# Deformable attention held by rows of four lines, with results and inputs moved during the loop and far lists regrouped through memory

## What is computed

```python
v = xt @ value_proj_w.T + value_proj_b
om = xt @ offset_mask_w.T + offset_mask_b
...
loc_x = px + DIL * kx + off[..., 0] * OFFSET_SCALE
loc_y = py + DIL * ky + off[..., 1] * OFFSET_SCALE
...
sampled = corner(y0i, x0i, (1 - wy) * (1 - wx)) + corner(y0i, x0i + 1, (1 - wy) * wx) + corner(y0i + 1, x0i, wy * (1 - wx)) + corner(y0i + 1, x0i + 1, wy * wx)
...
out = jnp.einsum('nhwkgc,nhwkg->nhwgc', sampled, mask_t)
out = out.reshape(N, L, C) @ output_proj_w.T + output_proj_b
```

## Time and profile before

| | us |
|---|---|
| median of 3 runs | 3287.48 (3285.68 to 3289.9) |
| profiled execution | 3290.47 |
| its span | 3288.8 |

### The profile page before, as it was taken

How to read it: one execution, slowest core, us unless ns; L and a number is a source line. 1 busy time by engine, 2 the same in 40 slices (tenths; PEclk the granted TensorE clock), 3 DMA queues, 4 the chain that set the end, 5 groups by cost and what they waited for, 6 DMA issues and landing times.

```text
span 3288.8 us, 77998 instructions
## 1 busy us (share of the span) xinstructions
PE 2733.5 (83%) x22424; PEld 2192.2 (67%) x22424; DVE 2719.8 (83%) x6553; ACT 1828.7 (56%) x3486; POOL 1162.0 (35%) x1557
## 2 busy tenths in 40 slices
PE   1888889999999999995677989998946799999986
PEld 0555555565565556564566888887835688888885
DVE  3888888888888888885667999999945799999996
ACT  0888888888888888884143443333202443334420
POOL 3333233333333333332446231346232441115550
PEclk9999999999999999998988999999978899999998
DMA  7889897888888898895553233333374433333334
GB/s 182 158 157 163 166 148 138 139 140 143 138 141 142 141 139 143 140 144 116 183 158 91 89 99 101 99 103 84 89 261 134 144 101 101 97 101 95 102 89 160
DMA packets 351779, 432.59 MB, mean 132 GB/s; under 512 B 42352, under 2 KB 275200, under 8 KB 346480
## 3 DMA queue, kind: packets, MB, share of 16 engines
q1 hardware_dynamic: 339696, 423.85, 58.5%
q0 software_dynamic: 11904, 6.44, 1.5%
HBM read 283.33 MB, written 147.09 MB: 131 GB/s over the span
## 4 chain that ended last, share of the span: by engine, by line
DVE 24%; issue 10%; DMA 6%; PE 5%; POOL 3%; DVEq 1%; ACT 1%; POOLq 1%; SPq 1%; ACTq 0%
DVE prod L1635 17%; DMA vring<-vals 3%; DVE tt L1619 2%; PE sum_ps L1429 2%; DVE my L1614 2%; DMA vring<-attended 1%; DVE x L1646 1%; PE sum_ps L1384 1%; ACT d_xn L1518 1%; DMA o_sel<-off_out,pos 1%; PE om_ps L1347 1%; POOL gath L1209 1%; PE sum_ps L1333 1%; POOLq L1216 1%; DMA out<-x 0%
## 5 line engine op out<-in xcount | busy, mean ns | idle before, releaser
L623 ACT ACTIVATE prob<-sbias,nmax 128x256 f32<-128x256 f32 x2048 | 903.9, 501 | 203.4 <-DVE nmax L716 201.0
L716 DVE CUSTOM_DVE_ANT_0 sbias<-s_ps,nbias 128x256 f32<-128x256 f32 x2048 | 768.0, 420 | 212.8 <-PE s_ps L508 201.4
L1635 DVE TENSOR_TENSOR prod<-vring,wt_ps 128x1920 f32<-128x1920 f32 (+3 forms) x512 | 898.8, 1815 | 18.8 <-DMA vring<-vals 11.9
L1384 PE MATMUL sum_ps<-d_ident,prod 128*128 128x128 f32 x6400 | 773.0, 279 | 83.5 <-DVE prod L1635 83.4
L1384 PEld LDWEIGHTS sum_ps<-d_ident,prod 128*128 128x128 f32 x6400 | 732.0, 144 | 131.8 <-DVE prod L1635 104.3
L521 PE MATMUL pt_ps<-a_ident,prob 128*128 128x128 f32 x4096 | 645.3, 280 | 140.5 <-ACT prob L623 137.5
L521 PEld LDWEIGHTS pt_ps<-a_ident,prob 128*128 128x128 f32 x4096 | 448.2, 141 | 284.3 <-DVE probT L725 134.3
L1484 ACT ACTIVATE hat<-off,one_col 128x576 f32<-128x576 f32 x128 | 140.7, 1099 | 700.6 <-DVE tt L1619 700.6
L508 PE MATMUL s_ps<-stack 96*128 96x256 bf16 x2048 | 396.6, 275 | 8.1 <-DMA stack<-parts_dram 7.4
L443 POOL CAST parts<-qk 128x1024 bf16<-128x1024 f32 x64 | 66.3, 1036 | 869.9 <-ACT qk L616 869.9
L725 DVE COPY probT<-pt_ps 128x512 f32<-128x512 f32 x512 | 351.9, 687 | 11.9 <-PE pt_ps L521 11.8
(11 more groups left out here) (170 smaller groups left out, 3382.2 us busy)
## 6 DMA issues: line engine op xcount, KB each, us to landing
stack<-parts_dram SPq DMA_DIRECT2D x768, 128.0 KB, 7.6
vring<-vals SPq DMA_DIRECT2D x270, 320.0 KB
parts_dram<-parts SPq DMA_DIRECT2D x64, 768.0 KB, 6.5
off_out<-off SPq DMA_DIRECT2D x64, 432.0 KB
strips<-x SPq DMA_DIRECT2D x68, 256.0 KB, 3.7
far_sums<-nothing SPq DMA_DIRECT2D x64, 256.0 KB, 2.1
attended<-on SPq DMA_DIRECT2D x256, 64.0 KB
x<-x SPq DMA_DIRECT2D x16, 1024.0 KB, 6.5
```

Source lines behind the costliest of these rows:

```text
L623: ins = nc.scalar.activation(prob[:, n % 4, half, :], sbias[:, n % SBIAS, half, :], ACT.Exp, bias=nmax[:, n % SBIAS, half:half + 1], scale ...
L716: ins = nc.vector.tensor_tensor_reduce(out=sbias[:, n % SBIAS, half, :], in0=s_ps[:, n % 2, half, :], in1=nbias[:, h, half, :], scale=1.0, ...
L1384: mm = nc.tensor.matmul(sum_ps[:, par, r * H:(r + 1) * H], prod[:, r % 2, dx, dy * C:(dy + 1) * C], ident[:], start=(r + dx + dy == 0), st ...
L1635: nc.vector.tensor_tensor(prod[:, r % 2, first:last].rearrange("p a (t c) -> p (a t) c", c=CG), vring[:, at:at + wide].rearrange("p a (t c ...
```

## The change

1. Groups hold four rows of the image (`lines`) instead of four columns (`cols`): the access to `x1` in the normalisations and in `result` becomes contiguous. A partition is then an x coordinate.
2. `found` takes the marks of a group; SP stores them to `key_out` in memory and loads an epoch's back as `keys`, so that a list is 16 neighbouring pixels of one row (`BLOCK`). `flags`, `count_far` and `read_counts` move to the next group, and `find_far` moves forward in its group.
3. SP stores a group's four rows during the loop (`store_lines`) and loads the next image's into the same place (`next_lines`). The first image's rows come in pieces of 256 KB between those of `attended`.
4. The normalised tiles of the value stage have four places (`xv`) instead of two.
5. Constants and weights of `deformable` are made and loaded within `attention` (`Fixed`, `fixed_tiles`, `fixed_bias`), and the zeros around `vals` are stored there.

The core of the diff:

```diff
+BLOCK = 16
+LINES = EPOCH * COLS
...
+XVS = 4
...
+def fixed_tiles(nc, pool, fixed, scratch, consts):
+
+
+    nc.gpsimd.memset(fixed.ones[:], 1.0).then_inc(consts, 1)
+    nc.gpsimd.memset(fixed.one_col[:, 0:1], 1.0).then_inc(consts, 1)
+    nc.gpsimd.memset(fixed.one_col[:, 1:2], -1.0).then_inc(consts, 1)
+    nc.gpsimd.memset(fixed.one_col[:, 2:3], 0.0).then_inc(consts, 1)
+    nc.gpsimd.memset(fixed.far_at[:].rearrange("p e i n -> p (e i n)"), 0).then_inc(consts, 1)
+    n_const = 5
...
+    made(nc.gpsimd.iota(whole[:, 0:KE], pattern=[[0, LINES], [1, KG]], base=1, channel_multiplier=KG))
+    made(nc.gpsimd.tensor_copy(scratch[:, KE:2 * KE], whole[:, 0:KE]))
+    made(nc.gpsimd.tensor_scalar(fixed.keytab[:], scratch[:, KE:2 * KE], pix, None, ALU.subtract))
...
+            for t, src in (*late_weights, (bom[:], b_om.partition_broadcast(P))):
+                sp.dma_start(t, src).then_inc(w_in, 16)
+            for col in (*range(PAD), *range(PAD + W, XP)):
+                sp.dma_start(at(vals, col * YP * C, [[NOTHING, YP * C // NOTHING], [1, NOTHING]]),
+                             nothing[0:YP * C // NOTHING, :]).then_inc(pad_out, 16)
...
+        xv = prod[:, 0].rearrange("p t c -> p (t c)")[:, 0:XVS * COLS * H].rearrange("p (s r y) -> p s r y", s=XVS, r=COLS)
...
-            for t, src in ((wproj_sb, w_proj), (wvalue_sb, w_value), (wom_sb, w_om), (wout_sb, w_out),
-                           (bout_sb, b_out)):
-                sp.dma_start(t[:], src).then_inc(w_in, 16)
-            for t, src in ((bproj_sb, bproj_row), (bvalue_sb, bv_row), (bom_sb, bom_row)):
-                sp.dma_start(t[:], src.partition_broadcast(P)).then_inc(w_in, 16)
-
-            sp.wait_ge(zeros_ready, count(1))
...
-                load_strip(0, 0, 0)
-                load_strip(1, 1, 0)
-                with sp.Fori(0, STRIPS // 2 - 1) as i:
-                    for par in range(2):
-                        load_attended(2 * i + par)
-                        load_strip(2 * i + par + 2, par, i + 1)
...
+                def store_lines(s):
+                    sp.wait_ge(res_ready, count(b * GROUPS + s.q + 1))
+                    if not isinstance(s.q, int):
...
+                    sp.dma_start(at(out, b * (C * PIX) + s.q * (COLS * W), [[PIX, P], [1, COLS * W]]),
+                                 x1[:, bass.ds(s.q * (COLS * W), COLS * W)]) \
+                      .then_inc(stored[s.place % 2], 16)
+
...
+                        sp.dma_start(x1[:, bass.ds(s.q * (COLS * W), COLS * W)],
+                                     at(x, (b + 1) * (C * PIX) + s.q * (COLS * W), [[PIX, P], [1, COLS * W]])) \
+                          .then_inc(x_in[n], 16)
...
+                if b == 0:
+                    for a in range(2):
+                        load_lines(0, a)
+                    for a in range(NA):
+                        load_attended(a)
+                        if a + 2 < NA:
+                            load_lines(0, a + 2)
+                else:
+                    for a in range(ATTS, NA):
+                        load_attended(a)
...
+                def store_found(s):
+                    n, par = b * GROUPS + s.q, s.place % 2
+                    sp.wait_ge(det_step, count(3 * n + 3))
...
+                    sp.dma_start(at(key_out[s.epoch_slot()], s.place % EPOCH * (COLS * W * KG), [[KG, P], [W * KG, COLS], [1, KG]]),
+                                 found[:, par]).then_inc(found_out[par], 16)
+
+                def load_keys(s):
+
+                    n = b * EPOCHS + s.epoch
+                    for par in range(2):
+                        sp.wait_ge(found_out[par], count(16 * (b * (GROUPS // 2) + EPOCH // 2 * (s.epoch + 1))))
+                        if not isinstance(s.q, int):
+                            sp.sem_inc(sp_passed, 1)
+                    sp.wait_ge(far_done, count(n + 1))
+                    if not isinstance(s.q, int):
+                        sp.sem_inc(sp_passed, 1)
+                    sp.wait_ge(keys_in, count(16 * n))
+                    if not isinstance(s.q, int):
+                        sp.sem_inc(sp_passed, 1)
+                    sp.dma_start(keys[:, s.epoch_slot()], at(key_out[s.epoch_slot()], 0, [[KE, P], [1, KE]])) \
+                      .then_inc(keys_in, 16)
...
+                        if r == 2 and s.has(LEAD):
+                            store_found(s.on(LEAD))
+                        if r == 2 and s.has(-RES_LAG - 1):
+                            store_lines(s.on(-RES_LAG - 1))
+                        if r == 3 and s.has(LEAD) and ends_epoch(s, LEAD):
+                            load_keys(s.on(LEAD))
+                        if r == 3 and s.has(-RES_LAG - 2) and b + 1 < B:
+                            next_lines(s.on(-RES_LAG - 2))
 
                 each_group(sp, columns)
                 load_far(first_spot(GROUPS - 1))
-                sp.wait_ge(res_ready, count((b + 1) * GROUPS))
...
+                if b + 1 < B:
+                    sp.wait_ge(prod_ready, count(2 * (b + 1) * W))
+                    for a in range(ATTS):
+                        sp.dma_start(att[:, a], at(attended, ((b + 1) * NA + a) * (COLS * W * C),
+                                                   [[C, P], [W * C, COLS], [1, C]])).then_inc(att_in[a], 16)
+                for q in range(GROUPS - RES_LAG - 1, GROUPS):
+                    store_lines(first_spot(q))
+                if b + 1 < B:
+                    for q in range(GROUPS - RES_LAG - 2, GROUPS):
...
-                    pool.wait_ge(v_done, count(b * GROUPS + v))
-                    pool.sem_inc(pool_passed, 1)
-                    if 2 <= v < AHEAD_OFF + 2:
-                        pool.wait_ge(om_done, count(b * GROUPS + v - 1))
+                    if v >= XVS:
+                        pool.wait_ge(v_done, count(b * GROUPS + v - XVS + 2))
                         pool.sem_inc(pool_passed, 1)
-                    nc.gpsimd.tensor_scalar(xn[:, 1], cols[:, v * COLS:(v + 1) * COLS, :], gn[:, 0:1], gn[:, 1:2],
+                        if v - XVS < AHEAD_OFF:
+                            pool.wait_ge(om_done, count(b * GROUPS + v - XVS + 1))
+                            pool.sem_inc(pool_passed, 1)
+                    nc.gpsimd.tensor_scalar(xv[:, v % XVS], lines[:, v * COLS:(v + 1) * COLS, :], gn[:, 0:1], gn[:, 1:2],
...
+                    if s.has(LEAD - 1) and ends_epoch(s, LEAD - 1):
+                        count_far(s.on(LEAD - 1).epoch)
...
-                    if u == 0:
-                        dve.wait_ge(far_done, count(b * EPOCHS + s.epoch + 1))
+                    dve.wait_ge(found_out[par], count(16 * (b * (GROUPS // 2) + s.half)))
...
-                        out=keys[:, s.epoch_slot(), u * KI:(u + 1) * KI].rearrange("p (r k) -> p r k", k=KG),
-                        in0=reach[:], scalar=1.0,
+                        out=found[:, par], in0=reach[:], scalar=1.0,
...
-                    dve.wait_ge(det_step, count(3 * (b * GROUPS + s.q) + 3))
+                    dve.wait_ge(keys_in, count(16 * (n + 1)))
...
-                    dst = cols[:, q * COLS:(q + 1) * COLS, :] if isinstance(q, int) else \
-                        cols[:, bass.ds(q * COLS, COLS), :]
+                    dst = lines[:, q * COLS:(q + 1) * COLS, :] if isinstance(q, int) else \
+                        lines[:, bass.ds(q * COLS, COLS), :]
...
-                    last_of_epoch = s.has(LEAD) and (s.place + LEAD) % EPOCH == EPOCH - 1
+                    ended = s.has(LEAD - 1) and ends_epoch(s, LEAD - 1)
                     products(s.q, par, 0)
+                    if ended:
+                        flags(s.on(LEAD - 1))
+                    if s.has(LEAD):
+                        find_far(s.on(LEAD))
                     products(s.q, par, 1)
                     if s.has(1):
                         tap_terms(s.on(1))
                     products(s.q, par, 2)
+                    if ended:
+                        read_counts(s.on(LEAD - 1))
                     if s.has(-RES_LAG):
                         result(s.on(-RES_LAG).q)
-                    if s.has(LEAD):
-                        find_far(s.on(LEAD))
-                    if last_of_epoch:
-                        flags(s.on(LEAD))
                     products(s.q, par, 3)
-                    if last_of_epoch:
-                        read_counts(s.on(LEAD))
```

360 lines of the change are left out of this document (187 added, 173 removed).

## The result

The changed kernel takes 3204.30 us (median of 4 runs, 3201.23 to 3205.39) against 3286.84 us (3285.68 to 3289.9): ratio 0.9746, 95% interval 0.9729 to 0.9763. Its profiled execution took 3204.88 us with a span of 3203.2; before, 3290.47 and 3288.8. So the trace has to explain 85.6 us. The prediction was 3210, with 77 less between the profiled executions.

What follows compares the result with a forecast made beforehand. VectorE was taken to bound the loop over groups. Gains of 157 us less 80 of added cost gave net -77; 3290.5 - 77 - 3 = 3210 us, range 3160 to 3262.

Steps and rivals of the forecast that it cites:

- loading of image 0: Start of the deformable half: x starts 11.6 us earlier and less work stands behind the last piece; -17 us.
- value stages, twice: Value stage of both images: four normalised tiles instead of two remove waits for the previous tile's matmuls; -34 us.
- between the images, with the projection: Lines move during the loop, so the 35.9 us gap shrinks to about 2 (-34); projection becomes VectorE's (-7).
- end: After the last result only one 256 KB store follows, 3.5 us instead of 22.9; -19 us.
- `result`, 64 times: VectorE's result addition loses its 512-byte step, 1.400 us becoming 0.684 as in L1548; -46 us.
- waits for far points, net of 24.3 before: Loops: 52 rounds instead of 40 make VectorE stall 96 us, against 24.3 before; +71 us.
- rest of the loops (exchange, contention): Loops: storing and loading the lists each epoch costs +3 us, contention of more transfers +6 us.
- What is queued behind?: SP's wait delays `fsum`, then turn, offset matmuls, `size` and `find_far`; mid-loop stalls: three rounds nothing, four 11.7, five 26.5 us.
- I am wrong if VectorE waits before MAX8: Sign against the forecast in the profile after: a VectorE wait before MAX8 would mean the keys come late.
- rival B: The key exchange is late, with pieces under 512 B below line rate; 3240 to 3280 us, chance 0.09.
- The +6 for the moved transfers: Loops: steady contention of more transfers with rounds and columns costs +6 us.
- Bias additions beside tap terms: Image 0's last three groups: POOL's additions and VectorE lock each other out, some 4 to 8 us; 2 taken.

Runs made afterwards that it cites:

- experiment 7: Changed kernel with all stores of results and all loads of the next image behind the loop instead of in it; 3280.19 us.
- experiment 6: Changed kernel with two places for the normalised tiles of the value stage instead of four; 3209.56 us.
- experiment 8: Changed kernel with additions like `result`, in different access patterns, appended after all is stored; 3218.70 us in one run, contiguous 0.75 us against 1.33 with the old step.
- experiments 1 and 2: Changed kernel with the number of rounds held to three, then to one, leaving out further far points of a list; 3145.74 us and 3119.47 us.
- Experiment 3: Changed kernel with SP's load of the far sum moved behind the load of the lists in the group where an epoch's search ends; 3229.45 us.
- experiment 4: Changed kernel with VectorE reading the counts ahead of P2, the third product, instead of behind it; 3201.36 us.

## Why the prediction was right

The time was right within 0.2%, and most of its terms were. Some of the closeness is luck: the value stages and `result` gave 11 us less than forecast, the waits and the rest of the loops cost 19 less. The table compares the profiled executions, landmark by landmark; the term for the loops is taken apart below it.

| term | predicted, us | measured, us |
|---|---|---|
| loading of image 0 (statistics' end 1609.39, now 1593.04) | -17 | -16.4 |
| value stages, twice | -34 | -27.3 |
| between the images, with the projection | -41 | -40.5 |
| end | -19 | -20.4 |
| `result`, 64 times | -46 | -42.1 |
| waits for far points, net of 24.3 before | +71 | +64 |
| rest of the loops (exchange, contention) | +9 | -3 |
| sum | -77 | -86 |

- **Loading, gap and end.** Each as worked out. That the gains of gap and end are real and not given back elsewhere is shown by experiment 7. No run takes the earlier loading (part 5) out.
- **Value stages.** An early step takes 3.13 us (3.2 forecast) and a late one 1.0 to 1.1 (1.1 forecast). What was missed is the exchange of the first lists: `flags` stands in this stage too, no product lies between its store and load, and MAX8 waits 3.15 and 3.41 us. I had priced the exchange in the loops only. And the step that I blamed for the old waits, two places, is the smaller part (experiment 6); the shorter reads probably do more.
- **`result`.** The cause is confirmed by experiment 8. It measures 742 ns and not 690, since I took its duration from L1548, another operation.
- **Far points.** 52 scatters, as counted. Three rounds in the middle take 53.7 to 55.2 us from the count to `fsum` (57.1 forecast), four 67.2 to 71.1 (71.9), five 82.2 (86.7). Waits by place, forecast and measured: loops' starts 14.3 and 14.3, measured 17.3 and 16.0; five rounds 26.5, measured 22.0; four in the middle of image 1 twice 11.7, measured 12.8 and 8.3; last epoch of image 0 15.9, measured 12.3; last of image 1 1.1, measured none. Together 96 and 88.7 (80.9 to 83.1 in experiments 6 to 8). Epochs of three rounds in the middle wait for nothing; SP stands 3.6 to 5.8 us in them (8 forecast), and VectorE has no wait there.
- **Slips in the working.** The terms of a group, 4 x 3.55 + 4.1 + 1.4 + 0.7, add up to 20.4 and not 19.9. The figure used was right all the same: a group without waits lasts 19.94 us (2000.98 to 2020.92), because the products start 3.47 apart. The way from `fsum` to the end of `size` is 9.8 in one sentence and 9.6 in the sum; it measures 9.6.
- **The step that failed** is "What is queued behind?". I listed what SP's wait holds (the columns, `fsum`) and left out what the change itself had put behind it, the store of the marks and the load of the lists. I had written that I am wrong if VectorE waits before MAX8; it does. The reason behind that sentence was rival B, a slow exchange, and that isn't it: experiments 1 and 2 show that the wait goes with the rounds. The size came out right because both chains end within 0.5 us of each other, which is luck of this layout. Experiment 3 shows the forecast chain, at 23.08 us in the same epoch.
- **Contention.** With one round VectorE has no wait before MAX8 in the loops, so the exchange by itself holds nothing up there. The +6 for the moved transfers isn't to be seen: experiment 7 has 7 us less in the loops, and experiments 6 and 8, which keep them, have 10 and 5 less. With the waits for rounds taken out, the three differ from the changed kernel by -1.5, -2.3 and +1.2 us. Why the rest of the loops comes out at -3 stays open; no experiment took it apart.
- **Bias additions beside tap terms.** The prediction took 2 us for them. In the profiled execution they cost 3.6 (1.69 instead of 1.05, 5.99 instead of 3.00), and `tt` has a mean of 1092 ns in image 0's loop against 1059. A bad execution pays 21 us at this place (experiment 4), far more than the 4 to 8 of the prediction: I let each of the four operations wait for one POOL instruction, and there one of them waited for many.
- **Why part 2 had to come with part 1.** Counted from the reference's own data, lists kept per partition in the new layout (one x, 16 rows) would hold 9 to 15 far points at most, since some x hold most of them; regrouped, it is 2 to 5. This is a count; such a kernel was not run.

## What to carry to other kernels

When a wait moves or a buffer passes through memory, write down the whole queue of the engine that waits, the new transfers included; the first of them that someone needs is the next bound. Where several chains start at one late event, moving one of them gains nothing (3229 us) and moving all of them does (3147 to 3153 us), and the next one may hide behind an order written for another purpose, like the weights here. Work moved beside another engine's must be looked at for what the two share: a wait that starts POOL's additions 14 us later delays nobody, and with it the multiplication of 22 us was gone from the trace. Before planning around buffers, look at the access pattern: a step of 16 bytes or more added 0.32 to 0.58 us to an addition of 0.75, with no wait to show for it. And before a few microseconds are put down to an edit, look at the same wait in runs that don't touch it.
